# Sixteen-head attention and a gated feed-forward: one half turn a unit goes by ScalarE and GpSimd

## The reference

```
scores = einsum('bhqd,bhkd->bhqk', q, k) * scale
attn   = softmax(scores, axis=-1)
x = layernorm(x + attention(x))
h = silu(lin(x, w1)) * lin(x, w2)
h = gelu(lin(h, h1)); h = gelu(lin(h, h2))
x = layernorm(x + lin(h, w3))
```

## Time and profile before

| | |
|---|---|
| profiled execution | 441.35 us, span 439.6 us |
| TensorE matmul busy | 426.9 us (97%) |
| VectorE busy | 383.8 us (87%) |
| ScalarE busy | 363.6 us (83%) |
| GpSimd busy | 106.9 us (24%) |
| granted TensorE clock, mean | 0.998 |

### The profile page before, as it was taken

How to read it: one execution, slowest core, us unless ns; L and a number is a source line. 1 busy time by engine, 2 the same in 40 slices (tenths; PEclk the granted TensorE clock), 3 DMA queues, 4 the chain that set the end, 5 groups by cost and what they waited for, 6 DMA issues and landing times.

```text
span 439.6 us, 9789 instructions
## 1 busy us (share of the span) xinstructions
PE 426.9 (97%) x3498; PEld 228.3 (52%) x3498; DVE 383.8 (87%) x704; ACT 363.6 (83%) x683; POOL 106.9 (24%) x198
## 2 busy tenths in 40 slices
PE   8999999999999999999999999999999899999995
PEld 3544545444444444444445454544333588877884
DVE  6799999999999999999999999999874576657636
ACT  4497989999998999998899998998799885678762
POOL 9730110101011010101101013958111363046103
PEclk9999999999999999999999999999999999999999
DMA  5667741111131111113011111121021000000101
GB/s 161 174 204 119 281 147 28 49 28 28 48 123 25 40 37 28 28 48 123 25 40 39 26 28 49 16 41 52 10 41 49 15 8 1 1 1 3 48 1 48
DMA packets 17117, 24.89 MB, mean 57 GB/s; under 512 B 5168, under 2 KB 9008, under 8 KB 16688
## 3 DMA queue, kind: packets, MB, share of 16 engines
q1 hardware_dynamic: 16464, 23.68, 19.8%
q10 hardware_dynamic: 608, 0.59, 0.5%
HBM read 15.08 MB, written 7.60 MB: 52 GB/s over the span
## 4 chain that ended last, share of the span: by engine, by line
PE 74%; DVE 12%; ACT 4%; SPq 3%; issue 2%; DMA 2%; POOL 1%; POOLq 0%; DVEq 0%; ACTq 0%
PE ps L1366 23%; PE ps L1288 18%; PE ps L1476 16%; DVE negmax L983 11%; PE ps L1350 9%; ACT arena L663 2%; DMA parts_q<-arena 2%; PE ps L1220 2%; PE ps L1231 1%; PE ps L1420 1%; PE ps L1316 1%; PE ps L1260 1%; SPq L462 1%; SPq L434 1%; ACT v_pad L716 1%
## 5 line engine op out<-in xcount | busy, mean ns | idle before, releaser
L983 DVE TENSOR_REDUCE negmax<-ps 128x1 f32<-128x512 f32 x458 | 274.5, 683 | 1.4 <-PE ps L1288 1.3
L663 ACT ACTIVATE arena<-ps 128x512 f32<-128x512 f32 x360 | 190.3, 605 | 21.3 <-PE ps L1350 14.7
L1350 PE MATMUL ps<-qx,kx 64*128 64x512 f32 x512 | 170.0, 450 | 0.9 <-DMA qx<-mT 0.6
L1288 PE MATMUL ps<-kx,qx 61*128 61x512 f32 x468 | 159.3, 440 | 0.8 <-DMA qx<-parts_q 0.5
L1288 PEld LDWEIGHTS ps<-kx,qx 61*128 61x128 f32 x468 | 75.1, 184 | 86.7 <-DVE negmax L983 76.6
L1366 PE MATMUL ps<-arena,v_pad 128*32 128x256 f32 (+3 forms) x1328 | 104.7, 407 | 2.4 <-ACT arena L663 2.4
L663 ACT ACTIVATE hf<-ps 128x512 f32<-128x512 f32 x152 | 83.3, 602 | 9.5 <-PE ps L1350 8.0
L1350 PEld LDWEIGHTS ps<-qx,kx 64*128 64x128 f32 x512 | 78.6, 184 | 18.2 <-ACT arena L663 11.5
L1476 PE MATMUL ps<-hid,w_high 128*128 128x512 f32 (+1 forms) x296 | 68.3, 387 | 0.8 <-issue 0.4
L1476 PEld LDWEIGHTS ps<-hid,w_high 128*128 128x128 f32 x296 | 54.2, 188 | 12.4 <-issue 0.8
L1366 PE MATMUL ps<-hf,v_pad 128*32 128x128 f32 (+1 forms) x600 | 47.5, 388 | 0.0
(11 more groups left out here) (109 smaller groups left out, 333.7 us busy)
## 6 DMA issues: line engine op xcount, KB each, us to landing
qx<-parts_q SPq DMA_DIRECT2D x60, 64.0 KB, 2.1
late_sb<-in_late SPq DMA_DIRECT2D x3, 1280.0 KB, 5.7
kx<-parts_k SPq DMA_DIRECT2D x56, 64.0 KB, 2.1
parts_q<-prt SPq DMA_DIRECT2D x3, 512.0 KB, 6.4
parts_q<-arena SPq DMA_DIRECT2D x3, 512.0 KB, 8.2
xT_sb<-in_xT SPq DMA_DIRECT2D x4, 256.0 KB, 4.0
xT_sb<-arena SPq DMA_DIRECT2D x28, 32.0 KB
prt<-den SPq DMA_DIRECT2D x7, 128.0 KB
```

Of the source, the lines that this page charges most:

```text
L663: nc.scalar.activation(probs(n // HG)[:, heads(n), :], ps[:, PLAN["score", n][0], :], ACT.Exp, scale=SCALE).then_inc(exp_done, 1)
L983: nc.vector.tensor_reduce(negmax[:, t // TURNS % 2, m % 2, h * QT + q:h * QT + q + 1], ps[:, MAX_BANK + m % 4, :], AX.X, ALU.max, negate=T ...
L1288: nc.tensor.matmul(ps[:, half_bank(m), :], qx[at, slot, qc, h, q * P:(q + 1) * P], kx[at, slot, h, part * C:(part + 1) * C], start=True, s ...
L1350: nc.tensor.matmul(ps[:, bank, :], kx[at, slot, h % PAIR, kt * P:(kt + 1) * P], qx[at, slot, qc, h % PAIR, :], start=True, stop=True)\
```

## The change

In each of the units 2 to 15, one half turn no longer goes to VectorE. It is the first half from the unit's eighth on that stands last in its group of three. ScalarE copies its bank out of PSUM with the sign turned, into `beside` (a part of `z`, free at that time). GpSimd folds the 512 columns to one by halving nine times; each halving is a subtraction, a minimum with zero and an addition. The result goes to the column of `negmax` that VectorE would have written. TensorE's ring waits for the copy where it waited for the maximum, and the counts of `max_taken` leave out these halves. The loops of VectorE and GpSimd over units are written out. The weight slices move from the last iteration to units 10 to 15, one before and one behind the split (unit 15: one), and the bias is added to `xres` behind the last split.

```diff
+def copied_halves():
+    halves = []
+    for u in range(2, U_ALL):
+        m = 2 * TURNS * u + BESIDE_FROM        # BESIDE_FROM = 8
+        while (m - AHEAD) % RUN != RUN - 1:
+            m += 1
+        halves.append(m)
+    return halves
+def taken(m):
+    return m - sum(n < m for n in BESIDE_HALVES)
...
 # ScalarE
+            def copy_beside(n):
+                m = BESIDE_HALVES[n]
+                act.wait_ge(max_scores, m + 1)
+                if n > 0:
+                    act.wait_ge(beside_step, BESIDE_STEPS * n)
+                nc.scalar.activation(beside[:], ps[:, half_bank(m), :], ACT.Copy, scale=-1.0)\
+                   .then_inc(beside_out, 1)
...
                     exp(n)
+                    if n == scores_of(g)[-1]:
+                        for m in turn_halves(g):
+                            if m in BESIDE_HALVES:
+                                copy_beside(BESIDE_HALVES.index(m))
...
 # GpSimd
+            def take_beside(u):
...
+                pool.wait_ge(beside_out, n + 1)
+                width = C // 2
+                while width:
+                    a, b = beside[:, 0:width], beside[:, width:2 * width]
+                    out = a if width > 1 else negmax[:, u % 2, m % 2, h * QT + q:h * QT + q + 1]
+                    nc.gpsimd.tensor_tensor(a, a, b, ALU.subtract).then_inc(beside_step, 1)
+                    pool.wait_ge(beside_step, done + 1)
+                    nc.gpsimd.tensor_scalar(a, a, 0.0, None, ALU.min).then_inc(beside_step, 1)
+                    pool.wait_ge(beside_step, done + 2)
+                    nc.gpsimd.tensor_tensor(out, a, b, ALU.add).then_inc(beside_step, 1)
+                    pool.wait_ge(beside_step, done + 3)
+                    done += 3
+                    width //= 2
...
-            for i in range(ITERS - 1):
-                split_max(i, 1)
-                split_max(i, 2)
...
+            def turn_maxima(u):
+                if u >= 2:
+                    take_beside(u)
+                if u >= W_UNIT:                        # W_UNIT = 10
+                    halve_w(2 * (u - W_UNIT))
+                g = u // QC + 1
+                if u % QC == 1 and 2 <= g < G_ALL:
+                    pool.wait_ge(pv_done, (g - 1) * QC * KT)
+                    stage_v(g, g % 2)
+                split_max(u)
+                if W_UNIT <= u < U_ALL - 1:
+                    halve_w(2 * (u - W_UNIT) + 1)
...
-            for k in range(STEPS):
-                if k % KT == 3 and k // KT + 1 < PER:
-                    split_max(ITERS - 1, k // KT + 1)
-                if k in W_STEPS:
-                    halve_w(W_STEPS.index(k))
-                if k == KT:
-                    pool.wait_ge(in_mid, 32)
-                    nc.gpsimd.tensor_tensor(xres[:], xres[:],
...
+            for u in range(1, U_ALL):
+                turn_maxima(u)
+            pool.wait_ge(in_mid, 32)
+            nc.gpsimd.tensor_tensor(xres[:], xres[:], bo_bc[:, :].unsqueeze(1).broadcast_to([P, TOK // P, D]),
+                                    ALU.add).then_inc(xres_ready, 1)
...
 # VectorE
-                dve.wait_ge(max_scores, i * (2 * PER * TURNS) + m + 1)
+                m += i * (2 * PER * TURNS)
+                dve.wait_ge(max_scores, m + 1)
...
+                if m in BESIDE_HALVES:
+                    return
...
 # TensorE
+                elif m - 4 in BESIDE_HALVES:
+                    pe.wait_ge(beside_out, BESIDE_HALVES.index(m - 4) + 1)
                 elif m >= 4:
-                    pe.wait_ge(max_taken, m - 3)
+                    pe.wait_ge(max_taken, taken(m - 3))
```

More of the change, by code:

```diff
@@ L68 @@
 FOLD = 5
+BESIDE_FROM = 8
+W_UNIT = 10
 TURN_AFTER, COPY_AFTER = 5, 6
@@ L161 @@
 PLAN = bank_plan()
+BESIDE_HALVES = copied_halves()
+def taken(m):
+    return m - sum(n < m for n in BESIDE_HALVES)
+BESIDE_STEPS = 3 * (C.bit_length() - 1)
 WO_BANK, X1T_BANK, INEXACT_BANK = [2, 3, 6, 7], [2, 3, 6, 7], 2
@@ L173 @@
 HF_STEPS = max(k for k in range(TAIL) if k % 3 == 2) + 1
-W_STEPS = (*range(0, 18, 2), 17, 18)
 STAGES = [(name, 2 * b + c) for b in range(B) for name in ("gate", "h1", "h2") for c in range(2)]
@@ L290, in build @@
         z = sb("z", [P, 2, TILES, D])
+        beside = z[:, 0].rearrange("p t d -> p (t d)")
         any_more = sb("any_more", [1, 1])
@@ L335, in build @@
         max_preset = sem("max_preset")
+        beside_out = sem("beside_out")
+        beside_step = sem("beside_step")
         max_merged = sem("max_merged")
@@ L804, in stage_v, with split_max @@
                     v_pad[:, slot, :, :, 0:DH],
-                    v_sb[:, :, :, :].rearrange("p g k (h d) -> p (g k) h d", h=HG)[:, g * KT:(g + 1) * KT, :, :]
+                    v_sb[:, :, :, :].rearrange("p g k (h d) -> p (g k) h d", h=HG)[:, bass.ds(g * KT, KT), :, :]
                 ).then_inc(v_staged, 1)
-            def split_max(i, w):
-                first = i is None
-                i = 0 if first else i
+            def split_max(w):
                 m, rest = (t.rearrange("p (r n) -> p r n", r=2)
-                           for t in (negmax[:, 0, 0, :] if first else negmin[:, w % 2, :], mrest[:]))
+                           for t in (negmax[:, 0, 0, :] if w == 0 else negmin[:, w % 2, :], mrest[:]))
                 none = zeros[:, :].rearrange("p (r n) -> p r n", r=2)
                 parts = mpart[:, w % 2, 0:PARTS * TURNS].rearrange("p (r i n) -> p i r n", r=2, i=PARTS)
[L816 to L823, removed]
+                done, merged = 3 * w, 3 * (w - 1)
+                pool.wait_ge(max_taken, taken((w + 1) * 2 * TURNS))
+                if w > 0:
                     nc.gpsimd.tensor_tensor(mrest[:], negmax[:, w % 2, 1, :], negmax[:, w % 2, 0, :], ALU.subtract)\
@@ L838, in split_max @@
                 nc.gpsimd.tensor_tensor(parts[:, 2], rest, parts[:, 1], ALU.subtract).then_inc(max_split, 1)
+            def take_beside(u):
+                n = u - 2
+                m, done = BESIDE_HALVES[n], BESIDE_STEPS * n
+                h, q = head_of(m // 2)
+                pool.wait_ge(beside_out, n + 1)
[11 more added lines that the diff above has]
+                    width //= 2
             pool.wait_ge(v_ready, 2)
@@ L853, in _ @@
             pool.wait_ge(rows_set, 4)
-            split_max(None, 0)
+            split_max(0)
             pool.wait_ge(v_ready, NC_)
@@ L1001, in turn_halves_from @@
                     turn_half(i, m)
-            with dve.Fori(0, ITERS - 1) as i:
+            for i in range(ITERS - 1):
                 turn_halves_from(i, 2 * WHOLE, 2 * WHOLE + 2 * PER * TURNS)
@@ L1330, in bank_free @@
                 else:
-                    pe.wait_ge(max_taken, n)
+                    pe.wait_ge(max_taken, taken(n))
             def turn_max(w):
@@ L1411, in out_proj @@
                     pe.wait_ge(in_mid, 32)
-                    pe.wait_ge(max_taken, 2 * U_ALL * TURNS)
+                    pe.wait_ge(max_taken, taken(2 * U_ALL * TURNS))
                 if c == 2:
```

10 lines of the change are left out of this document (1 added, 9 removed).

## The result

The changed kernel takes 447.12 us (median of five runs, 446.03 to 447.76), against 441.21; the ratio is 1.0125, with an interval of 1.0106 to 1.0144. The forecast was 442.9, with a range of 438.6 to 445.5. The change makes the kernel slower by 5.9 us; the interval lies clear of no change. The direction is as forecast. The time lies above the range.

A forecast was written before the change was run, and what follows sets the result against it. The prediction took VectorE's half-turn maxima as the bound, with TensorE following closely. From the profiled 441.35 us it took 2.9 for skipped maxima and added 4.4 for the delayed normalisation: 442.85, predicted as 442.9, range 438.6 to 445.5.

The forecast's parts named there:

- The first normalisation waits for the add: Start of the tail: GpSimd's xres add starts first and holds the shared ports; VectorE's normalisation comes 4.4 us late.
- Rival 1: Start of the tail: the normalisation wins the ports, TensorE's transposes of x1 lose some 0.4 us; 438.9 us, chance 0.22.
- The row that the forecast took for it: Profile row: VectorE's L1118 took 1.40 us beside a GpSimd instruction, its fellow 0.66; read as waiting to that instruction's end.
- rival 2: Tail: TensorE's clock drops in the gap before the output projection; 0 to 2.4 us lost, 444.6 us with 1.7; chance 0.19.
- the waits of every unit so far left the clock at 1.00: Argument against the clock drop, from TensorE's waits in the units, though none was as long as the forecast gap.
- stays low for as long again as the gap, 4.9 us at half pace: Assumed length of TensorE's low clock after the gap in the tail; 0 to 2.4 us lost, by the author's estimate.
- Fourteen copies come to ScalarE ... Price nothing.: Units 2 to 15: copies of 0.52 us each hide in ScalarE's spare 1.7 us per unit; at worst 7 us.
- Gain where a half is skipped, 2.9 us: VectorE at the 14 skipped halves: 8.4 us of work goes, but waiting for TensorE leaves 2.9 us; ends 0.8 and 8.4.
- Before the unit ends VectorE is the bound again: Units 2 to 15: TensorE wins 0.11 us a group, 0.77 us up to the next change, so the gain is kept.
- The fold: GpSimd: 27 dependent steps per unit, 10.3 to 10.8 us; unit 11's split up to 0.6 us late, priced at nothing.
- Loops written out: no price: VectorE's last four units are already written out and the last takes 19.13 us like those in the loop; no cost.

The follow-up runs named there:

- e1: The changed kernel with the xres add on GpSimd waiting until both first normalisations on VectorE are done; 441.36 us.
- e6: The changed kernel with the xres add at its place, as four instructions of 512 columns instead of one of 2048; 442.49 us.
- e3: The changed kernel with ScalarE copying only 8 of the 512 columns of each skipped half, GpSimd folding as before; 444.97 us.
- after: The changed kernel itself, with the whole change, as set against the kernel without it; 447.12 us.
- e8b: e1 with ScalarE copying each of the 14 halves twice, first to a place that nobody reads; 447.67 us.
- before: The kernel without the change, to which all ratios are taken; 441.21 us.
- e4: The changed kernel without copy and fold, all maxima on VectorE; the new places of the weights and the add stay; 447.28 us.
- e9: The changed kernel with the add after both first normalisations, weight slices behind the splits, and all maxima on VectorE again; 441.63 us.

## Why the prediction was wrong

- *The first normalisation waits for the add.* Right: 4.98 us measured, +4.31 at the output projection against 4.4 forecast. e1 and e6 show the cause. Rival 1, the other order, did not happen. The row that the forecast took for it did not settle it, though: 1.40 us in place of 0.66 is also about twice as long, as with a port that is divided. The 4.98 us decide.
- *The clock (rival 2).* This is the step that failed in the tail. The forecast's sum has no term for it, since "the waits of every unit so far left the clock at 1.00"; rival 2 had 0.19. The clock fell in the gap, and cost 2.7 us in the profile, 2.0 by the medians. Rival 2 itself was near, with 1.7 taken and 2.4 as its bound, but "stays low for as long again as the gap, 4.9 us at half pace" was too short: it stayed low about 6 us into the new work, and the scores that ScalarE's run waits for stand behind the projection and its products on TensorE.
- *"Fourteen copies come to ScalarE ... Price nothing."* This is the step that failed in the main part. I took ScalarE's 1.7 us of spare time per unit for cover. What counted was TensorE's third score of the group behind, which needs a bank that the delayed exponential frees: the copy's length costs 1.9 us over 13 units (e3 against after), and a second copy 6.3 (e8b against e1).
- *Gain where a half is skipped, 2.9 us.* Right that VectorE goes over to waiting for TensorE (0.41 us at unit 10), but the places win 1.3 us. "Before the unit ends VectorE is the bound again" failed. In unit 10 of before, VectorE holds TensorE back, with groups 1.80 us apart; in after they go on at TensorE's own pace, 1.68 to 1.72, up to its last group. So TensorE does not get back the lead that the forecast read from before, and it reaches the next place with less. With the copy almost taken out (e3), 2.2 us are won over 13 units against e4, still 0.7 under the forecast. That last part is argued from these paces, and no run separates it further.
- *The fold.* Its 27 steps in unit 10, from 203.52 to the end of the last one, take 10.9 us, forecast 10.3 to 10.8. The split of unit 11 comes late as forecast, and costs the 0.2 us that I took as nothing.
- *Loops written out: no price.* Right: with all maxima on VectorE, e4 and e9 take 249.81 and 249.80 us for the 13 units, against 249.73.
- *Sum.* Forecast: -2.9 + 4.4 = +1.5. Measured over the spans: -0.25 in the 13 units, +4.31, +2.68, and -0.3 at the start and the end: +6.4. The miss of 4.9 us is 2.7 for the clock and 2.65 for the main part (1.9 the copies, the 0.2 of GpSimd's lateness within them, the rest the size of the gain), less 0.4 at the add and the two ends. The profiled execution is the slowest of its five; in the median the miss is 4.2.

## What to carry to other kernels

Spare time of an engine is no cover by itself: look for the buffer that its next instruction frees, and at how long the engine behind can wait for that. Where an instruction is moved to a place where the other of VectorE and GpSimd has its one urgent piece of work with two SBUF inputs, the urgent one may wait for all of it; let the moved one wait, or cut it into pieces. Where an edit leaves TensorE empty, look at the granted clock behind the gap too: here it cost another 2.0 to 2.7 us on top of 4.3.

## What the runs showed of the hardware

- A VectorE instruction with two inputs in SBUF and a GpSimd instruction that reads SBUF exclude each other here for whole instructions: 0.69 us became 4.98 beside a 4.51 us add that had started 0.07 us earlier, and 1.75 beside pieces of the same add. It also holds for a bfloat16 addition on VectorE (e1: three additions 6.67 us in place of 2.41), and for a comparison with one input, float32 to bfloat16 (e1: the add, started behind it, 6.50 in place of 4.51).
- A gap of 4.8 us on TensorE was followed by 6 us of new work at a granted clock of 0.50; the cost was 2.7 us, and 2.0 and 2.1 in e3 and e4. With 20 small products in the gap (recorded as 40) it stayed at 1.00.
- On GpSimd the fold's steps take 0.74 us at 256 columns with two inputs and 0.85 with one and constants, 0.19 and 0.22 at one column.
